# Third expert stage: result blocks stored whole and gathered by slot during the full attention; second expert product in three float16 terms

## The reference, cut to what matters

```python
x = x + 0.5 * moe0(layernorm(x))        # expert stage 0: 8 experts, top 2, hidden 256, silu(x w1) * (x w3), then w2
x = x + window_attention(layernorm(x))  # 16 heads of 8, window 32
x = x + 0.5 * moe0(layernorm(x))        # expert stage 1, the same weights
x = x + 0.5 * moe1(layernorm(x))        # expert stage 2: 8 experts, top 2, hidden 512, gelu(x W1 + b1) W2 + b2
x = x + full_attention(layernorm(x))    # with a residual of its own norm, 512 x 512 scores per head
x = x + 0.5 * moe1(layernorm(x))        # expert stage 3, the same weights as stage 2
```

## Time and profile before

| | |
|---|---|
| median of 3 runs | 3271.73 us (3268.25 to 3272.54) |
| the profiled execution | 3283.67 us, of which 3281.6 us span |
| PE, DVE, POOL, ACT busy | 75%, 54%, 50%, 45% of the span |
| routers(0) | 0 to 244 us |
| expert stage 0 | 244 to 478 us |
| windowed attention, with its prologue | 478 to 1144 us |
| expert stage 1 | 1144 to 1403 us |
| routers(2) | 1403 to 1622 us |
| expert stage 2 | 1625 to 1906 us |
| prologue of the full attention | 1906 to 1964 us |
| full attention, steps 0 to 15 | 1964 to 2879 us |
| expert stage 3 | 2921 to 3219 us |
| last combine and the output | 3219 to 3281 us |

### The profile page before, as it was taken

One profiled execution on the slowest core, in us unless ns is written; L12 is line 12 of the kernel. 1 busy time (PEld: TensorE's weight loads), 2 busy tenths in 40 slices (PEclk: granted clock), 3 DMA queues, 4 the chain that ended last, 5 costly groups with the idle time before them and its releaser, 6 DMA issues.

```text
span 3281.6 us, 68666 instructions
## 1 busy us (share of the span) xinstructions
PE 2466.4 (75%) x22942; PEld 1670.0 (51%) x22942; DVE 1778.9 (54%) x5466; ACT 1469.6 (45%) x3114; POOL 1642.8 (50%) x1870
## 2 busy tenths in 40 slices
PE   2227766989899577722398859999999999958881
PEld 1226654767777466622297723333333333348771
DVE  3433325766676433266422158888888888722214
ACT  1213323544555333311254417776777777734440
POOL 5765554566664445557554452445455451234441
PEclk9999987999999799955599969999999999979996
DMA  7122222222222142232222220111111111022225
GB/s 161 46 62 74 81 77 78 74 71 81 75 63 70 36 125 80 73 91 89 59 78 66 65 80 29 49 42 45 51 40 59 35 43 36 14 55 68 63 63 164
DMA packets 264267, 222.49 MB, mean 68 GB/s; under 512 B 66279, under 2 KB 244461, under 8 KB 263405
## 3 DMA queue, kind: packets, MB, share of 16 engines
q1 hardware_dynamic: 229372, 146.98, 16.5%
q0 software_dynamic: 34560, 71.11, 6.8%
HBM read 114.00 MB, written 107.53 MB: 68 GB/s over the span
## 4 chain that ended last, share of the span: by engine, by line
PE 60%; DVE 11%; issue 10%; ACT 6%; DMA 4%; another core or an unknown queue 4%; SPq 3%; POOL 2%; ACTq 0%; POOLq 0%; DVEq 0%
PE PS L498 16%; PE PS L589 9%; PE PS L502 7%; PE PS L678 7%; PE PS L647 5%; PE PS L626 5%; ACT arena L826 3%; DVE xr L1192 2%; PE PS L630 2%; PE PS L696 2%; PE PS L634 2%; DVE mxs L1392 2%; PE PS L524 2%; PE PS L655 1%
## 5 line engine op out<-in xcount | busy, mean ns | idle before, releaser
L1069 POOL DMA_INDIRECT slot_inputs<-xs,slots x512 | 510.1, 996 | 706.2 <-PE PS L647 377.4
L926 ACT ACTIVATE arena<-PS 128x512 f32<-128x512 f32 (+1 forms) x1344 | 698.8, 586 | 289.3 <-PE PS L647 152.6
L1078 POOL DMA_INDIRECT choice_outputs<-arena x568 | 545.6, 961 | 554.7 <-DVE arena L1349 249.7
L1392 DVE TENSOR_REDUCE mxs<-PS 128x1 f32<-128x512 f32 x1024 | 651.1, 684 | 121.4 <-PE PS L626 114.6
L626 PE MATMUL PS<-w,q 96*128 96x512 f16 x1024 | 395.3, 388 | 15.3 <-DVE mxs L1392 12.1
L647 PE MATMUL PS<-q,w 100*128 100x512 f16 x1024 | 388.1, 381 | 18.5 <-ACT arena L926 18.1
L1349 DVE TENSOR_TENSOR arena<-PS,arena 128x256 f16<-128x256 f32 x284 | 119.5, 421 | 440.1 <-ACT arena L826 354.4
L826 ACT ACTIVATE arena<-PS 128x256 f16<-128x256 f32 (+2 forms) x586 | 258.6, 451 | 222.0 <-PE PS L502 139.7
L884 ACT ACTIVATE arena<-PS,b1c 128x256 f32<-128x256 f32 x568 | 224.0, 489 | 298.8 <-PE PS L498 215.0
L1395 DVE TENSOR_REDUCE mxs<-PS 128x2 f32<-128x320 f32 x512 | 245.6, 488 | 182.1 <-PE PS L634 174.7
L502 PE MATMUL PS<-ident,arena 128*128 128x128 f32 x1084 | 199.0, 286 | 116.5 <-DMA arena<-slot_inputs 92.1
(11 more groups left out here) (180 smaller groups left out, 3943.0 us busy)
## 6 DMA issues: line engine op xcount, KB each, us to landing
arena<-slot_inputs SPq DMA_DIRECT2D x284, 129.0 KB
G<-choice_outputs SPq DMA_DIRECT2D x128, 256.0 KB
qk_parts<-qk SPq DMA_DIRECT2D x64, 256.0 KB, 2.2
q<-qk_parts SPq DMA_DIRECT2D x128, 96.0 KB
choice_outputs<-arena POOLq DMA_INDIRECT x568
slot_inputs<-xs,slots POOLq DMA_INDIRECT x512
qk_parts<-qk SPq DMA_DIRECT2D x64, 128.0 KB, 2.2
W<-qk_parts SPq DMA_DIRECT2D x128, 48.0 KB
```

Of the source, the lines that this page charges most:

```text
L926: activate(pT[:, u % PTR, 0:n], PS[:, SC0 + u % NSC[a], 0:n], ACT.Exp, scale=SCALE).then_inc(s_pe, 1)
L1069: g.indirect_dma_start(Xs, bass.IndirectOffsetOnAxis(ap=slots[:, s, c, k:k + 1], axis=0), xs[:, n % XSR, c, k], None).then_inc(s_scat[c][n ...
L1078: g.indirect_dma_start(Yt, bass.IndirectOffsetOnAxis(ap=xid[:, b % XRING, j, D:D + 1], axis=0), yb[:, b % YRING, j], None).then_inc(s_ysc[ ...
L1392: vec.tensor_reduce(mxs[:, m % 2, p % NT, QROWS + col:QROWS + col + 1], PS[:, MX0 + u % NMX], AX, ALU.max)\
```

## The change

- Second product (`down`), all expert stages: the input is split into a float16 head and rest in a new tile `hh` (ring of 2), the weights w2 and W2 too (times 64, as the others); three terms in float16, so 12 products of 128 columns for a block in stages 0 and 1 and 24 in stages 2 and 3, in the place of 4 and 8 in float32. ACT copies the head (512 columns; in stages 2 and 3 the other 512 heads are copied by DVE), DVE subtracts (512 or 1024 columns), both in a new function `parted`, called for block b - 1 between `turned(b + 1)` and the activation or gate of block b. The activation of block b in stages 2 and 3 now waits for the rest of block b - 2 in place of `down(b - 2)`. Evictions get a factor 1/64.
- The weights w2 are staged as a third piece beside w1 and w3, ACT waits for all three; W2 comes in four pieces of its own, so there are eight in `ffn(1)`.
- Expert stage 2 only (BYBLOCK): SP stores each result block whole to a new table `block_outputs` (12 loads later in its own order), and POOL scatters nothing: its call of `ffn(2)` is gone. The input ring is freed when block b - 8 is turned. DVE computes for each row the place of its results in that table, once (`rows_in_blocks`). In `routers(2)` the second choice is scattered from the first copy.
- Full attention: the rows of sequence t + 4 are gathered by POOL, 8 indirect DMAs a sequence, at named positions between the scatters, which are moved to other positions; the 8 of sequence 0 stand before the first step. Nothing of this is fetched by SP.
- The tile `vt` is cleared by DVE.

```diff
@@ SP, ffn(f)
-                for b in range(NBLK):
+                for b in range(NBLK + STLAG):
+                    if f == BYBLOCK and b >= STLAG:
+                        n = b - STLAG
+                        sp.wait_ge(s_yev, blk(f, n))
+                        sp.dma_start(Ys[n * BS:(n + 1) * BS].rearrange("(p j) d -> p j d", j=BJ), yb[:, n % YRING])\
+                          .then_inc(s_yst[n % YRING], 16)
...
-                    if b >= XRING:
+                    if b >= XRING and f != BYBLOCK:
                         sp.wait_ge(s_ysc[b % XRING], block_done(f, b - XRING))
+                    elif b >= XRING:
+                        sp.wait_ge(s_tx, blk(f, b - XRING))
@@ PE, ffn(f)
                 def down(b):
-                    pe.wait_ge(s_gt if f < 2 else s_act, blk(f, b))
+                    pe.wait_ge(s_hl, blk(f, b))
                     if b >= 2:
                         pe.wait_ge(s_yev, blk(f, b - 2))
...
+                    for c in range(C):
+                        for k, (iv, ih) in enumerate([(0, 0), (0, 1), (1, 0)]):
+                            for j in range(BJ):
+                                at = c * BS + j * P
+                                ins = mm(PS[:, YB + b % 2, j * D:(j + 1) * D], hh[:, b % 2, ih, at:at + P],
+                                         V[:, iv, bass.ds(off[b] + c * P, P)], start=c == 0 and k == 0 and j == 0,
+                                         stop=c == C - 1 and k == 2 and j == BJ - 1)
@@ ACT, routers(f) and ffn(f)
-                        router_second(f, i)
+                        if f == 0:
+                            router_second(f, i)
...
                         if i == 2:
                             eng.wait_ge(s_stg, 16 * len(big))
...
                     if b >= 2:
-                        eng.wait_ge(s_y, blk(f, b - 2))
+                        eng.wait_ge(s_hl, blk(f, b - 2))
...
+                def parted(b):
+                    eng.wait_ge(s_gt if f < 2 else s_act, blk(f, b))
+                    if b >= 2:
+                        eng.wait_ge(s_y, blk(f, b - 2))
+                    h = hact[:, b % 2, 2 * BS:4 * BS] if f < 2 else hact[:, b % 2, 0:2 * BS]
+                    copy(hh[:, b % 2, 0, 0:2 * BS], h).then_inc(s_hi, 1)
@@ DVE, ffn(f)
+                def parted(b):
+                    if f < 2:
+                        v.wait_ge(s_hi, blk(f, b))
+                        vec.tensor_tensor(hh[:, b % 2, 1, 0:2 * BS], hact[:, b % 2, 2 * BS:4 * BS], hh[:, b % 2, 0, 0:2 * BS],
+                                          ALU.subtract).then_inc(s_hl, 1)
+                        return
+                    v.wait_ge(s_act, blk(f, b))
                     if b >= 2:
                         v.wait_ge(s_y, blk(f, b - 2))
+                    link(vec.tensor_copy(hh[:, b % 2, 0, 2 * BS:4 * BS], hact[:, b % 2, 2 * BS:4 * BS]))
+                    v.wait_ge(s_hi, blk(f, b))
+                    vec.tensor_tensor(hh[:, b % 2, 1], hact[:, b % 2], hh[:, b % 2, 0], ALU.subtract).then_inc(s_hl, 1)
@@ POOL, attention(a)
-                step(g.memset(vt[:], 0.0))
+                def rows_in(s, i):
+                    c, k = i // NT, i % NT
+                    if s >= 2:
+                        pool.wait_ge(s_cmb, nth(fc, s - 2))
+                    g.indirect_dma_start(G[:, s % 2, k, c], None, Ys,
+                                         bass.IndirectOffsetOnAxis(ap=places[:, s, c, k:k + 1], axis=0))\
+                     .then_inc(s_gsl[s % 2], 16)
...
+                for k in range(YRING):
+                    pool.wait_ge(s_yst[k], block_stored(last_in(k, YRING)))
+                pool.wait_ge(s_plc, 1)
+                for i in range(2 * NT):
+                    rows_in(0, i)
                 for t in range(-3, SEQS + 2):
                     if t >= 0 and valid(t + 3):
                         combine(fc, t + 3)
-                    rows_out(t, [(3, 0, 0), (4, 0, 1)])
+                    r_in(t, 0, 0)
+                    r_in(t, 1, 1)
+                    r_in(t, 2, 2)
+                    r_out(t, 3, 0)
+                    r_in(t, 4, 3)
                     if valid(t + 3):
+                        p_rstd(t + 3)
+                        p_norm(t + 3)
+                    r_out(t, 5, 1)
...
+                    r_in(t, 6, 4)
+                    r_out(t, 7, 2)
+                    r_out(t, 8, 3)
...
             routers(2)
-            ffn(2)
             attention(1)
@@ DVE, rows_in_blocks and attention(a)
+                link(vec.tensor_tensor(past, bcast(at, E - 1), bcast(ebase[:, 1:E], n, 1), ALU.is_ge))
+                link(vec.tensor_tensor(past, past, bcast(tdel[:, 0:E - 1], n, 1), ALU.mult))
+                link(vec.tensor_reduce(back[:], past, AX, ALU.add))
...
+                link(vec.memset(vt[:], 0.0))
```

More of the change, by code:

```diff
@@ L855, in routers @@
                             eng.wait_ge(s_stg, 16 * len(big))
-                        copy(big[i - 2][1][:, 0], stage[:, i - 2], WS).then_inc(s_hs, 1)
+                        copy(big[i - 2][1][:, 0], stages[i - 2], WS).then_inc(s_hs, 1)
                     if i >= 8 and i - 8 < KR and f % 2 == 0:
@@ new lines, in r_out, with p_rstd, p_norm @@
+                def r_out(t, p, i, part=0):
+                    if valid(t - 2):
+                        to(t, p, part)
+                        scatter(fr, t - 2, i // NT, [i % NT])
+                def p_rstd(n):
+                    pool.wait_ge(s_pvar, nth(a, n))
+                    g.tensor_tensor(rs[:, n % 2], ve[:, n % 2], mhalf[:], ALU.pow).then_inc(s_prs, 1)
+                def p_norm(n):
+                    pool.wait_ge(s_prs, nth(a, n))
+                    if nth(a, n) > 1:
+                        pool.wait_ge(s_xt, nth(a, n) - 1)
+                    for k in range(NT):
+                        ins = g.tensor_scalar(xn[:, k], xr[:, n, k], mv[:, n % 2, k, 0:1], rs[:, n % 2, 1, k:k + 1],
+                                              ALU.subtract, ALU.mult)
+                    ins.then_inc(s_pxn, 1)
@@ new lines, in p_residual @@
+                def p_residual(n):
+                    step(g.tensor_tensor(xz[:, 0], mv[:, n % 2, :, 0], rs[:, n % 2, 0], ALU.mult))
+                    step(g.tensor_scalar(xz[:, 1], rs[:, n % 2, 0], 1.0, None, ALU.add))
+                    pool.wait_ge(s_pxn, nth(a, n))
+                    for k in range(NT):
+                        ins = g.tensor_scalar(xr[:, n, k], xr[:, n, k], xz[:, 1, k:k + 1], xz[:, 0, k:k + 1],
+                                              ALU.mult, ALU.subtract)
+                    ins.then_inc(s_xz, 1)
@@ new lines, in r_outs, with local_steps @@
+                def r_outs(t, parts):
+                    for p, i in parts:
+                        r_out(t, p, i)
+                def local_steps(t):
+                    if t >= 0 and valid(t + 3):
+                        combine(fc, t + 3)
+                    r_outs(t, [(3, 0), (4, 1)])
+                    if valid(t + 3):
+                        p_rstd(t + 3)
+                        p_norm(t + 3)
+                    r_outs(t, [(6, 2), (7, 3), (8, 4)])
+                    if valid(t - 1):
+                        router_rstd(fr, t - 1)
+                        router_norm(fr, t - 1, range(NT))
+                    r_outs(t, [(11, 5), (12, 6), (14, 7)])
@@ L1471, in late @@
                         router_diff(fr, t - 1)
+                v.wait_ge(s_tx, blk(fc, NBLK - 1))
+                if not full:
+                    for k in range(XRING):
+                        v.wait_ge(s_ysc[k], block_done(fc, last_in(k, XRING)))
+                link(vec.memset(vt[:], 0.0))
+                vec.memset(vt[:, :, :, :, DH:DH + 1], 1.0).then_inc(s_one, 1)
                 if not full:
```

176 lines of the change are left out of this document (100 added, 76 removed).

## The result

The changed kernel takes 3251.4 us (median, 3244.3 to 3257.5) against 3271.4 us of the kernel before on the same chip: a ratio of 0.9937, 95% interval 0.9920 to 0.9954. A second set gave 3248.0 us, 0.9928 (0.9911 to 0.9944). The forecast was 3208 us, 43 us lower. Its direction was right, its size was not; 3251 lies inside the range, but in rival B's part of it.

What follows compares the result with a forecast made beforehand. No engine was full (PE busiest, 75%), so each stage had its own limit; -49 + 15 + 6 - 45 + 4.5 + 4 = -64 us gave 3219 us profiled, a median of 3208 us; 8-in-10 range 3165 to 3288 us.

Steps and rivals of the forecast that it cites:

- rival B: Stage 3 keeps its slow beat of 8.53 to 9.1 us for two blocks; 3261 us in all, chance 0.32.
- Stage 2 by blocks: Stage 2 without POOL's scatters: PE's sequencer sets 3.2 us a block, 232 us in place of 281, -49 us.
- Into the full attention: Prologue of the full attention: store landing and gathers delay the first combine to 14.3 us, +15 us in all.
- Stage 3: Expert stage 3, scatters kept: late signals no longer reach PE's products, 3.5 us a block for 58 blocks, -45 us.
- A: The main forecast, stage 3 at 3.5 us a block: median 3208 us, own range 3180 to 3236, chance 0.42.
- Steps of the full attention: 12 steps of the full attention get 8 gathers more, +0.5 us each: +6 us, bounds 0 and 36.
- C: Full attention: doubled indirect DMAs cost 12 steps up to 36 us, steps of 60 us or more; 3291 us, chance 0.15.
- The Trainium skill's rule: Stage 3: DVE's float32 SBUF copy holds POOL's descriptor port, so scatters start late by up to the copy's length.
- Second product: Stages 2 and 3: float16 products take PE 2.87 us a block; sequencer steps make it 3.2, bounds 2.87 and 3.4.
- stages 0 and 1: Expert stages 0 and 1 are beaten by POOL and keep their beat: +4 us together, bounds -15 to +20.
- weights: Staging before stage 0: ACT waits for w2 too, +3.5 us, and 1 more for the third split.
- The distance of median and profile: Whole kernel: the median was taken to lie 12 us below the profiled execution, as before the change.

Runs made afterwards that it cites:

- experiment 2: Last scatter of each full-attention step moved from position 15 to 14, on the changed kernel: 3228.7 us, ratio 0.9872.
- experiment 5: Changed kernel, scatter at position 14, gathers before residual, plus POOL pauses: 0.45 us per scatter pair 3203.5 us, 0.2 us per scatter 3217.0; changed kernel rerun 3248.0.

## Why the prediction was right or wrong

*Stage 2 by blocks:* right, -47 against -49, and for the stated reason: 3.14 us a block by the sequencer (forecast 3.2), shown by the fixed addresses (2.88 us, where PE's products are the limit).

*Into the full attention:* right. The first combine starts 14.0 us after the last result (1857.64 to 1871.69), and the term is +15.7 against +15. In part this is luck: 2.4 of the 15 us stood for late signals, for which no row was given, and what follows the first combine grew by 9.3 us against the 6 that were reasoned out.

*Stage 3:* mis-sized by 20 us. "A late signal of up to 1.3 us reaches neither PE's next first product nor its second" was true of the gelu (139 us of waits in 249 us, 3 in 200) and false of the kernel. The turned block is the next to be awaited, its signal too is raised while scatters run, and it comes mostly 2.1 to 2.6 us late, at most 3.4. I had freed one waiter and not asked who stands next; the trace of the kernel before could have told, since that signal was late there in 26 of 71 blocks. 3.7 us a block is between A's 3.5 and B's 4.27.

*Steps of the full attention:* mis-sized by 13 us. "+0.5 x 12" priced the indirect DMAs, which cost 0 (step 2, and all steps of experiment 2). What cost 1.0 us a step was a moved neighbour: the last scatter went from position 14 to 15, the combine behind it ran into DVE's routing sums, and in five steps the granted clock followed. The steps of 60.4 us met C's sign ("60 or more"), by another mechanism than C's, a late signal: experiment 2 has as many indirect DMAs and lost nothing. C's 36 us was also more than its own figures give: 12 x 2.6 = 31.

*The Trainium skill's rule* (SBUF - State Buffer, "SBUF: two separate sides") was weighed for a copy in SBUF. Its other half, that a DVE instruction with two SBUF inputs and a GpSimd one that reads SBUF exclude each other for the whole of an instruction, is what the traces show: 0.19 to 1.18 us for DVE's sum, 0.96 to 1.86 us for a scatter, both gone when the overlap or the second input goes. The half that spoke for B shows little here: of the 53 scatters of stage 3 that start under DVE's copy to float16, 46 take 0.96 us and 7 up to 1.22. That section of the Trainium skill would have pointed to the fault in the steps; I had looked at stage 3 alone, where the halved subtraction shows no price of it that can be measured.

*Second product* (2.88 us of PE a block) and *stages 0 and 1* were within their bounds; the *weights* cost about 2 us (4.5 forecast), by experiment 5. (The 3.6 us a block that the prediction gives for stage 1 was its whole window of 259 us; from rest to rest it took 234.0 us, stage 0 233.1, both 3.3 a block.) *The distance of median and profile* was carried over from one execution, and was worth 12 us of the miss.

## What to carry to other kernels

When an order of work on one engine is changed, look at every instruction that is pushed later, not only at the ones added: here one scatter moved by one position cost 19 us in ten steps, eight added gathers a step cost nothing. When a wait is removed from a loop that a late signal drives, name the next waiter of the same signal source before pricing the gain. A part that helps in its own stage (47 us) may be paid back in the stages that take over its work; run each part alone before keeping both.

## What the runs showed of the hardware

- A DVE sum of two SBUF inputs (0.19 us) beside a POOL addition in SBUF took 1.18 us; a scatter of 0.96 us begun under such a DVE operation of 1.23 us took 1.86 us, at most 2.02 (25 of 38 took over 1.0); with one input in PSUM, 0.96.
- PE idle for 1.6 us was followed, in five steps of ten, by about 3 us at a granted clock of 0.52 and a loss of 1.4 to 3.1 us. Idle for 0.62 us at the same place, in experiment 2, the clock stayed at 1.00 in each of steps 2 to 12.
- PE's signals come mostly 1 to 3 us late in many blocks while POOL issues indirect DMAs closely (turned blocks of stage 3: 31 of 71); 16 rows instead of 128 leave it at 32, pauses of 0.49 us behind each pair at 20. In stage 2, without them, no turned block was late by over 0.3 us. What in the issue holds them stays open.
- PE's sequencer needs about 0.125 us for each distinct address from a register: eight fewer of them took 0.26 us off a block (3.14 to 2.88), until PE's products were the limit.
